# One-hots of 64 columns and a tenth run without gathers in a graph network on one core

## The chip, the cores and the metric

The kernel runs on one core of a Trainium2 chip, as one launch. The metric is the device time of that launch in microseconds (us), as the median of several runs; less is better.

## The reference

The graph has 6250 nodes with 128 features and 100000 edges, `src[e]` to `dst[e]`, sorted by `dst`. Two layers of a graph convolution come first, then a graph attention layer. Each of the two is added to its input and normalised by row.

```python
def gcn_conv(x, src, dst, ew, W, b):          # with self loops of weight 1
    deg = segment_sum(ew, dst)
    dinv = where(deg > 0, rsqrt(deg), 0)
    norm = dinv[src] * ew * dinv[dst]
    return segment_sum((x @ W)[src] * norm[:, None], dst) + b
x = layernorm(x + sigmoid(gcn_conv(relu(gcn_conv(x, .., W1, b1)), .., W2, b2)))
z, rh = x @ fc_w.T, edge_attr @ fc_r_w.T
e = leaky(z[src] @ a0 + z[dst] @ a1 + rh @ a2)
alpha = exp(e - max over dst) / sum over dst
x = layernorm(x + relu(segment_sum(alpha * (z[src] + rh), dst) + z @ loop_w))
```

## The kernel before

**Tiles, groups, banks.** Edges are cut into T = 782 tiles of 128, eight to a group (GT = 8, G = 98 groups). As `dst` is sorted, a tile's edges go to few neighbouring nodes. `base(t)` is the first of the W = 128 nodes that tile t may reach, and `rankC` holds each edge's node less that base. Sums over nodes are matmuls: the gathered rows of a tile (128 edges by 128 features) are the weights, the moving operand is a one-hot matrix S (128 edges by 128 nodes) with the edge's weight at its rank. They accumulate in a PSUM bank that holds 384 nodes and an overhang; there are NA = 17 such banks, each closed by six groups.

**Setup.** Rows of indices are turned into columns, the degrees are summed with bf16 one-hots `SH` (VectorE makes three groups of four, L1571; ScalarE the fourth, L1191 and L1195; matmuls L811), and the features are scaled by `dinv` and stored. `find_odd` (L1545 to L1562) tests whether any rank lies outside 0 to 127; if so a slow fallback runs behind everything else.

**Three passes.** Pass 0 and pass 1 are the two convolution layers, pass 2 the attention layer. GpSimd fetches the source rows, one indirect DMA for a tile (L720), into a ring of R = 18 groups (12 in pass 2). It waits for the group that it overwrites to be summed. VectorE makes S for each group (`build_S`, L1608), up to four groups ahead of TensorE; TensorE sums the eight tiles (`sum_group`, L858, in pass 2 also L860 for the edge attributes). A closed bank goes through ScalarE (`evacuate`, L1215), TensorE (`layer`, L932) and VectorE to memory; the next pass starts gathering when all banks of the one before are stored.

**Sets without gathers.** A run of 32 tiles (a set) can do without gathers, since the node rows lie in SBUF (`rows`, 49 buckets of 128 nodes). Nine sets are sorted in pass 0 by the source's bucket, four groups each, from step `MAKE[s]` on: `make_hi` (VectorE, L1627), `count_before` (TensorE, L870 to L874), `make_ranks` (VectorE, L1634 to L1650), `permute` (TensorE, L885), and at the end `unpack` (VectorE), `turn_low` (TensorE, L891), `store_low` (ScalarE). Six of them replace gathers in pass 0, all nine in pass 1, so pass 0 has 74 steps (one group each) and pass 1 has 62; three replace gathers in pass 2 in another way. A set's rows are then looked up four buckets (a chunk) at a time: SP loads the low source bits (L535), ScalarE makes a one-hot of them (`slot_onehot`, L1239 and L1241), TensorE looks up (`look_up`, L898), ScalarE copies (`copy_looked`, L1232), VectorE makes one-hots over 288 nodes (`make_slots`, L1681), TensorE sums (`sum_slots`, L910). After 13 chunks ScalarE copies the set's sum (`copy_set`, L1256) and TensorE adds it to the bank (`add_sets`, L919) in the step in which that bank closes.

The order on each engine is written out by hand, step by step; `CHUNK_AT` gives the step of each chunk, `MAKE` the first step of each set's sorting. TensorE in a step of pass 0:

```python
for m in chunks_at(0, h - 1): look_up(m)
for s_, g in made_at(h, 0): count_before(s_, g)
for s_, g in made_at(h, 3):
    if g == ST // GT - 1: turn_low(s_)
add_sets(0, h)
sum_group(0, h)
for m in chunks_at(0, h - 1): sum_slots(m)
```

VectorE in the same step: `make_hi`, `build_S`, `make_ranks`, `make_slots`, `unpack`. ScalarE: copies of the chunks of the step before, then the one-hots of this step's chunks. In pass 1 VectorE and TensorE also pick the node scores of the attention layer for each group (L1825, L944), two groups a step (`picks_at`); 72 groups are done in the pass, 26 between pass 1 and pass 2.

## Time and profile before

| | us |
|---|---|
| median of 3 runs | 2409.7 (2406.36 to 2409.96) |
| span of the profiled execution, its own time | 3348.6 |
| busy in it: TensorE, its weight loads | 2044.2, 1762.3 |
| busy: VectorE, ScalarE, GpSimd | 1834.8, 946.7, 1718.9 |
| matmuls of the groups: L858 3540, L860 1564 | 672.5, 340.3 busy |
| indirect DMAs (L720): 144 and 446 tiles in pass 0, 494 in pass 1, 686 in pass 2 | 1770 in all |

The profiled execution is one run under the profiler, and it is longer than the runs that are timed; nothing lies around its span. In the trace PE is TensorE, PEld its weight loads, DVE VectorE, ACT ScalarE, POOL GpSimd and SP the queue of loads; "L858" is a line of the kernel. A float32 matmul appears as two matmuls with two weight loads, so a group of eight tiles is x16. In brackets stands how long the engine was idle before, and what ended that.

### The profile page before, as it was taken

The page shows a single profiled execution, that of the slowest core. Times are in us where ns is not written, and L with a number is a line of the kernel's source. Part 1 is how long each engine was busy: PE and PEld are TensorE (multiplying, and loading weights), DVE is VectorE, ACT ScalarE, POOL GpSimd, SP SyncE. Part 2 cuts the span into 40 slices and gives each one's busy share as a digit, 9 for nine tenths or more (in the row PEclk, how much of TensorE's full clock was granted, in tenths as well). Part 3 has the DMA queues.
Part 4 walks back from the last instruction along what each step waited for, and adds up shares of the span by engine and source line. Part 5 has one row for each costly group of instructions (what it writes and reads, how often), then busy time and mean ns, then how long its engine had stood idle before and what let it go on. Part 6 is the DMA issues. An engine that isn't in the chain of part 4 may idle for free.

```text
span 3348.6 us, 40819 instructions
## 1 busy us (share of the span) xinstructions
PE 2044.2 (61%) x13384; PEld 1762.3 (53%) x13384; DVE 1834.8 (55%) x7005; ACT 946.7 (28%) x1754; POOL 1718.9 (51%) x1781
## 2 busy tenths in 40 slices
PE   1416444588888911177777888106677667756786
PEld 1315433566767811166666677005666666645675
DVE  3626435577779810156656687217654564546457
ACT  1316000122233300033333444101254225412541
POOL 7351666665550067466556500555766646663640
PEclk9857667798999955588988899557778778877888
DMA  4112221222221122123333332525343534443431
GB/s 118 30 42 66 69 61 47 61 61 63 60 62 32 51 76 53 41 74 86 99 103 102 93 91 80 138 62 147 97 103 97 134 93 102 108 117 79 103 97 34
DMA packets 272093, 270.54 MB, mean 81 GB/s; under 512 B 43454, under 2 KB 218709, under 8 KB 271862
## 3 DMA queue, kind: packets, MB, share of 16 engines
q1 hardware_dynamic: 201790, 143.87, 15.1%
q0 software_dynamic: 56640, 117.52, 14.8%
q10 hardware_dynamic: 13448, 6.47, 0.7%
q8 instruction: 112, 1.84, 0.2%
q14 instruction: 103, 0.84, 0.1%
HBM read 254.14 MB, written 13.97 MB: 80 GB/s over the span
## 4 chain that ended last, share of the span: by engine, by line
PE 35%; DVE 21%; another core or an unknown queue 21%; issue 15%; ACT 4%; SPq 1%; DMA 1%; POOL 1%; ACTq 0%; DVEq 0%; POOLq 0%
PE ps L858 9%; PE ps L910 8%; DVE SR L1608 5%; PE ps L860 3%; PE ps L898 3%; PE ps L1045 2%; DVE U L1709 2%; DVE SR L1681 2%; DVE SR L1571 1%; PE ps L885 1%; DVE U L1648 1%; PE ps L1029 1%; POOL ring L720 1%; PE ps L792 1%
## 5 line engine op out<-in xcount | busy, mean ns | idle before, releaser
L720 POOL DMA_INDIRECT ring<-x_d,srcC x1132 | 1109.7, 980 | 971.2 <-issue 579.0
L858 PE MATMUL ps<-SR,ring 128*128 128x128 f32 x3540 | 672.5, 320 | 205.0 <-issue 132.0
L858 PEld LDWEIGHTS ps<-SR,ring 128*128 128x128 f32 x3540 | 580.5, 231 | 238.9 <-issue 178.9
L720 POOL DMA_INDIRECT ring<-h_d,srcC x494 | 469.9, 951 | 457.1 <-DMA h_d<-Lb 170.9
L1681 DVE TENSOR_SCALAR SR<-iota_r,cols 128x288 f32<-128x288 f32 x735 | 365.0, 564 | 303.9 <-remote 226.6
L910 PE MATMUL ps<-SR 128*128 128x288 f32 x1470 | 416.6, 435 | 118.1 <-ACT SR L1232 75.3
L910 PEld LDWEIGHTS ps<-SR 128*128 128x128 f32 x1470 | 292.3, 205 | 212.7 <-ACT SR L1232 77.5
L860 PE MATMUL ps<-SR 128*128 128x128 f32 x1564 | 340.3, 312 | 40.8 <-issue 34.6
L1232 ACT COPY SR<-ps 128x512 f32<-128x512 f32 (+1 forms) x195 | 106.0, 561 | 758.4 <-remote 502.9
L860 PEld LDWEIGHTS ps<-SR 128*128 128x128 f32 x1564 | 279.6, 228 | 48.3 <-issue 48.0
L898 PE MATMUL ps<-rows,SR 128*128 128x128 f32 x1470 | 196.2, 285 | 122.5 <-ACT SR L1241 90.6
L898 PEld LDWEIGHTS ps<-rows,SR 128*128 128x128 f32 x1470 | 186.7, 200 | 134.0 <-ACT SR L1241 96.0
L1608 DVE TENSOR_SCALAR SR<-iota,rankC,ewC 128x128 f32<-128x128 f32 x940 | 253.3, 357 | 2.6 <-DVE U L1812 1.1
L1608 DVE TENSOR_SCALAR SR<-iota,rankC,cols 128x128 f32<-128x128 f32 x782 | 213.0, 355 | 14.7 <-issue 11.7
L720 POOL DMA_INDIRECT ring<-in_x_dram,srcC x144 | 137.3, 953 | 93.7 <-issue 90.5
L1571 DVE TENSOR_SCALAR SR<-iota_h,rankC 128x128 bf16<-128x128 bf16 x584 | 107.6, 260 | 125.9 <-issue 106.1
L1709 DVE SCALAR_TENSOR_TENSOR U<-SR,v2B 128x128 f32<-128x128 f32 x686 | 156.0, 286 | 34.3 <-DVE U L1709 18.1
L1239 ACT ACTIVATE SR<-SR,negp 128x512 bf16<-128x512 bf16 (+1 forms) x195 | 134.9, 692 | 112.0 <-remote 100.3
L811 PE MATMUL ps<-SR,cols 128*3 128x128 bf16 (+2 forms) x974 | 74.0, 237 | 110.7 <-issue 57.0
L1241 ACT ACTIVATE SR<-SR,negp 128x512 f32<-128x512 bf16 (+1 forms) x195 | 135.9, 697 | 6.4
L1963 DVE TENSOR_TENSOR_SCAN U<-U,ps 32x384 f32<-32x384 f32 (+2 forms) x27 | 25.4, 942 | 203.8 <-remote 115.7
L811 PEld LDWEIGHTS ps<-SR,cols 128*3 128x3 bf16 x974 | 60.0, 96 | 123.5 <-issue 65.0
(288 smaller groups left out, 2703.4 us busy)
## 6 DMA issues: line engine op xcount, KB each, us to landing
SR<-in_edge_attr_dram SPq DMA_DIRECT2D x97, 512.0 KB
SR<-low_d SPq DMA_DIRECT2D x90, 256.0 KB
U<-dlo_d SPq DMA_DIRECT2D x74, 256.0 KB
ring<-x_d,srcC POOLq DMA_INDIRECT x1132
ring<-h_d,srcC POOLq DMA_INDIRECT x494
SR<-dlo_d SPq DMA_DIRECT2D x12, 512.0 KB
ring<-in_edge_attr_dram SPq DMA_DIRECT2D x12, 512.0 KB
U<-lo_d SPq DMA_DIRECT2D x18, 256.0 KB
```

The source lines that it names most:

```text
L720: pool.indirect_dma_start(ring[:, ring_at(p, h if p < 2 else q), k, 0:width], None, (x if p == 0 and h < R0 else table)[:, :], bass.Indire ...
L811: last = nc.tensor.matmul(ps[6 + k % 2][0:3, lo:hi], ewP[:, t, :], SH[:, q % ND, j, w0:w0 + hi - lo], start=False, stop=t == LAST[k])
L858: last = nc.tensor.matmul(ps[(p * NA + k) % 2][:, at], ring[:, ring_at(p, h), j, 0:D], S[:, gg % NS, j, :], start=False, stop=stop)
L860: last = nc.tensor.matmul(ps[2 + k % 2][:, at], rh[:, q % NR, j, :], S[:, gg % NS, j, :], start=False, stop=stop)
L898: last = nc.tensor.matmul(ps[3 + m % 2][:, i * P:(i + 1) * P], ohS[:, m % 2, i * P:(i + 1) * P], rows[:, a, 0:D], start=True, stop=True)
L910: nc.tensor.matmul(ps[5][:, SLACK:SPAN], rowX[:, m % 2, i * P:(i + 1) * P], slotS[:, n % NQ, :], start=False, stop=a == NB - 1).then_inc(s ...
L1239: nc.scalar.activation(low, low, ACT.Abs, bias=negp[:, 0:1]).then_inc(s("low_apart"), 1)
L1241: return nc.scalar.activation(out, low, ACT.Relu, bias=negp[:, 1:2], scale=-1.0)
L1571: last = v.tensor_scalar(SH[:, q % ND, j, :], iota_h[:, :], rankC[:, t:t + 1], None, ALU.is_equal)
L1608: last = v.tensor_scalar(S[:, gg % NS, j, :], iota[:, :], rankC[:, t:t + 1], w[:, t:t + 1], ALU.is_equal, ALU.mult)
L1681: v.tensor_scalar(slotS[:, n % NQ, :], iota_up, slotD[:, RUNS[i], a:a + 1], slotW[:, RUNS[i], a:a + 1], ALU.is_equal, ALU.mult).then_inc(s ...
L1709: v.scalar_tensor_tensor(junk[:, n % NJ, :], attr, 1.0, v2B[:, :], ALU.mult, ALU.mult, accum_out=s2C[:, t:t + 1]).then_inc(s("rh_dotted"), 1)
```

## The change

For all but the first and the last eight tiles the one-hots are made, and the matmuls run, over the 64 columns 32 to 95 of the 128 (`view`); the test in `find_odd` uses the same bounds. Ten sets are sorted in place of nine, starting every 5 or 6 steps in place of 6, and pass 1 uses ten, which leaves it 58 steps; its chunks come at 5 steps for 12 in place of 57 for 117. Beside that: the second set buffer moves to another tile; ScalarE makes the one-hot of chunk m + 2 right after it copies chunk m; VectorE makes ranks ahead of the high parts and of S; `turn_low` moves to the end of the step before; up to four picks in a step where many are ready; the table of one bank's node scores is made after pass 1 and not in it.

```diff
+NEAR, EDGE = W // 4, GT
...
+def view(t):
+
+    return (NEAR, W - NEAR) if EDGE <= t < T - EDGE else (0, W)
...
 
     b, out = base(t), []
-    for k in range(b // BW, (b + W - 1) // BW + 1):
-        lo, hi = max(b, k * BW), min(b + W, (k + 1) * BW)
+    a, z = (b + w for w in view(t))
+    for k in range(a // BW, (z - 1) // BW + 1):
+        lo, hi = max(a, k * BW), min(z, (k + 1) * BW)
...
-SETK = (6, 8, 10, 12, 14, 15, 2, 4, 9)
-USED = ((0, 1, 2, 3, 4, 5), (6, 7, 0, 1, 8, 2, 3, 4, 5))
+SETK = (6, 8, 10, 12, 14, 15, 2, 3, 4, 11)
+USED = ((0, 1, 2, 3, 4, 5), (6, 7, 8, 0, 1, 2, 9, 3, 4, 5))
...
-NQ = 15
+NQ = 16
...
-CHUNK_AT = [[29 + m * 40 // (N0 * NC) for m in range(N0 * NC)], [1 + m * 57 // (len(USED[1]) * NC) for m in range(len(USED[1]) * NC)]]
-MAKE = [17 + 6 * i for i in range(NSET)]
+CHUNK_AT = [[29 + m * 40 // (N0 * NC) for m in range(N0 * NC)], [1 + m * 5 // 12 for m in range(len(USED[1]) * NC)]]
+MAKE = [17 + 11 * i // 2 for i in range(NSET)]
...
-        first, done = done, max(done, min(ready // 2 * 2, done + 2)) if i < HS[1] - 6 else done
+        first, done = done, max(done, min(ready // 2 * 2, done + (4 if ready - done > 12 else 2))) if i < HS[1] - 6 else done
...
-        cols = sb("cols", [P, max(2 * TC + 2, 2 * SPAN + 2 * NSET * NB)])
+        cols = sb("cols", [P, max(2 * TC + 2, SPAN + 2 * NSET * NB)])
...
-        setsum = cols[:, 0:2 * SPAN].rearrange("p (a n) -> p a n", a=2)
-        slotD, slotW = (cols[:, 2 * SPAN + k * NSET * NB:2 * SPAN + (k + 1) * NSET * NB].rearrange("p (s a) -> p s a", a=NB) for k in range(2))
+        slotD, slotW = (cols[:, SPAN + k * NSET * NB:SPAN + (k + 1) * NSET * NB].rearrange("p (s a) -> p s a", a=NB) for k in range(2))
...
+        setsum = (cols[:, 0:SPAN], Lb[:, 4, P:P + SPAN])
...
-                    at, stop = slice(column(t), column(t) + W), t + 1 in OPENS or t + 1 == T and p < 2
+                    lo, hi = view(t)
+                    at, stop = slice(column(t) + lo, column(t) + hi), t + 1 in OPENS or t + 1 == T and p < 2
                     if near:
-                        last = nc.tensor.matmul(ps[(p * NA + k) % 2][:, at], ring[:, ring_at(p, h), j, 0:D], S[:, gg % NS, j, :], start=False, stop=stop)
+                        last = nc.tensor.matmul(ps[(p * NA + k) % 2][:, at], ring[:, ring_at(p, h), j, 0:D], S[:, gg % NS, j, lo:hi], start=False, stop=stop)
                     if p == 2:
-                        last = nc.tensor.matmul(ps[2 + k % 2][:, at], rh[:, q % NR, j, :], S[:, gg % NS, j, :], start=False, stop=stop)
+                        last = nc.tensor.matmul(ps[2 + k % 2][:, at], rh[:, q % NR, j, :], S[:, gg % NS, j, lo:hi], start=False, stop=stop)
...
-                for s_, g in made_at(h, 3):
-                    if g == ST // GT - 1:
-                        turn_low(s_)
                 add_sets(0, h)
                 sum_group(0, h)
                 for m in chunks_at(0, h - 1):
                     sum_slots(m)
+                for s_, g in made_at(h, 2):
+                    if g == ST // GT - 1:
+                        turn_low(s_)
...
                 for j, t in enumerate(tiles(q)):
-                    last = nc.scalar.activation(SH[:, q % ND, j, :], iota_h[:, :], ACT.Abs, bias=rankC[:, t:t + 1], scale=-1.0)
+                    lo, hi = view(t)
+                    last = nc.scalar.activation(SH[:, q % ND, j, lo:hi], iota_h[:, lo:hi], ACT.Abs, bias=rankC[:, t:t + 1], scale=-1.0)
...
-                nc.scalar.activation(SH[:, q % ND, 0:n, :], SH[:, q % ND, 0:n, :], ACT.Relu, bias=ones[:, 0:1], scale=-1.0).then_inc(s("deg_onehot_act"), 1)
+                nc.scalar.activation(SH[:, q % ND, 0:n, lo:hi], SH[:, q % ND, 0:n, lo:hi], ACT.Relu, bias=ones[:, 0:1], scale=-1.0).then_inc(s("deg_onehot_act"), 1)
...
+                if i == 1:
+                    act.wait_ge(s("dlo_stored"), 16)
                 at = act.value_load(shift[0:1, RUNS[i]:RUNS[i] + 1], min_val=0, max_val=SLACK)
-                nc.scalar.copy(setsum[:, i % 2, :], ps[5][:, bass.ds(at, SPAN)]).then_inc(s("set_copied"), 1)
+                nc.scalar.copy(setsum[i % 2], ps[5][:, bass.ds(at, SPAN)]).then_inc(s("set_copied"), 1)
...
             def set_copies(p, h):
                 for m in chunks_at(p, h - 1):
                     copy_looked(m)
+                    if m + 2 < (len(RUNS) if p else N0) * NC:
+                        slot_onehot(m + 2)
...
             for h in range(HS[0]):
-                set_copies(0, h)
-                for m in chunks_at(0, h):
-                    slot_onehot(m)
                 for s_, g in made_at(h, 3):
                     if g == ST // GT - 1:
                         store_low(s_)
+                set_copies(0, h)
+                if h == CHUNK_AT[0][0]:
+                    slot_onehot(0)
+                    slot_onehot(1)
...
-                for m in chunks_at(1, h):
-                    slot_onehot(m)
+                if h == CHUNK_AT[1][0]:
+                    slot_onehot(N0 * NC)
+                    slot_onehot(N0 * NC + 1)
...
-                link(v.tensor_scalar(tmpC, rankC[:, :], 0.0, None, ALU.is_lt))
+                for a, z in ((0, EDGE), (EDGE, T - EDGE), (T - EDGE, TC)):
+                    last = v.tensor_scalar(tmpC[:, a:z], rankC[:, a:z], float(view(a)[0]), None, ALU.is_lt)
...
-                link(v.tensor_scalar(tmpC, rankC[:, :], float(W), None, ALU.is_ge))
+                for a, z in ((0, EDGE), (EDGE, T - EDGE), (T - EDGE, TC)):
+                    last = v.tensor_scalar(tmpC[:, a:z], rankC[:, a:z], float(view(a)[1]), None, ALU.is_ge)
...
-                    last = v.tensor_scalar(SH[:, q % ND, j, :], iota_h[:, :], rankC[:, t:t + 1], None, ALU.is_equal)
+                    lo, hi = view(t)
+                    last = v.tensor_scalar(SH[:, q % ND, j, lo:hi], iota_h[:, lo:hi], rankC[:, t:t + 1], None, ALU.is_equal)
...
-                    last = v.tensor_scalar(S[:, gg % NS, j, :], iota[:, :], rankC[:, t:t + 1], w[:, t:t + 1], ALU.is_equal, ALU.mult)
+                    lo, hi = view(t)
+                    last = v.tensor_scalar(S[:, gg % NS, j, lo:hi], iota[:, lo:hi], rankC[:, t:t + 1], w[:, t:t + 1], ALU.is_equal, ALU.mult)
...
+                for s_, g in made_at(h, 1):
+                    make_ranks(s_, g)
                 for s_, g in made_at(h, 0):
                     make_hi(s_, g)
                 build_S(0, h, wraw if h < R0 else ewC)
-                for s_, g in made_at(h, 1):
-                    make_ranks(s_, g)
...
-                        node_table(k)
+                        if k < NA - 4:
+                            node_table(k)
...
-                for k in (NA - 3, NA - 2, NA - 1):
+                for k in (NA - 4, NA - 3, NA - 2, NA - 1):
```

## Rows read from the trace of the kernel before

**Rows 1.** The chain that ended last, shares of the span by engine.
```profile
PE 35%; DVE 21%; another core or an unknown queue 21%; issue 15%; ACT 4%; SPq 1%; DMA 1%; POOL 1%; ACTq 0%; DVEq 0%; POOLq 0%
```
**Rows 2.** Timeline, early pass 1: start us, us, engine, line, operation, tiles, count, idle before.
```profile
1201.21 3.75 PE L858 MATMUL ps<-SR,ring 128*128 128x128 f32 x16 [5.12 <-DMA ring<-h_d,srcC]
...
1215.76 0.37 PE L898 MATMUL ps<-rows,SR 128*128 128x128 f32 x1 [2.43 <-issue]
...
1218.57 0.37 PE L898 MATMUL ps<-rows,SR 128*128 128x128 f32 x1 [2.43 <-issue]
```
**Rows 3.** Busy us by stretch: stretch, length, PE, PEld, DVE, ACT, POOL (counts), clock, DMA, GB/s.
```profile
25.00:296.00 271.00, 94.20 (x1091) 76.73 (x1091) 118.89 (x608) 84.90 (x213) 122.32 (x130) 0.77 0.17 44
...
1006.00:1177.00 171.00, 151.24 (x1029) 131.84 (x1027) 143.95 (x449) 58.01 (x108) 2.17 (x3) 0.97 0.14 42
...
3241.00:3349.00 108.00, 76.35 (x541) 69.80 (x541) 78.41 (x328) 20.22 (x38) 0.47 (x1) 0.86 0.17 48
```
**Rows 4.** Timeline, gathers of pass 1 (72 of them from the first to the second row).
```profile
1199.79 0.94 POOL L720 DMA_INDIRECT ring<-h_d,srcC  x1 [0.30 <-issue]
...
1289.65 0.94 POOL L720 DMA_INDIRECT ring<-h_d,srcC  x1 [0.30 <-issue]
```
**Rows 5.** Timeline, one step of pass 1 after the last gather.
```profile
1971.50 0.55 PE L944 MATMUL ps<-U 128*128 128x3 bf16 x16
...
1971.90 2.03 PE L858 MATMUL ps<-SR,ring 128*128 128x128 f32 x16
...
1972.75 3.93 DVE L1681 TENSOR_SCALAR SR<-iota_r,cols 128x288 f32<-128x288 f32 x8
...
1973.77 4.05 PE L910 MATMUL ps<-SR 128*128 128x288 f32 x16
...
1976.60 2.13 DVE L1608 TENSOR_SCALAR SR<-iota,rankC,ewC 128x128 f32<-128x128 f32 x8
...
1977.65 1.95 PE L898 MATMUL ps<-rows,SR 128*128 128x128 f32 x16
...
1979.44 0.55 PE L944 MATMUL ps<-U 128*128 128x3 bf16 x16
```
**Rows 6.** Waits of GpSimd in pass 1, 1389 to 2078: total us, times, longest.
```profile
POOL ring L720 <- PE ps L858: 115.4, 25, 29.4
```
**Rows 7.** Two widths on VectorE: one line's durations (min/median/max ns), one group of instructions.
```profile
L1617 DVE SCALAR_TENSOR_TENSOR U<-iota,rankC x9: 179/183/189, 497.7 to 1104.6; 128x32 f32<-128x32 f32 x9
...
L1709 DVE SCALAR_TENSOR_TENSOR U<-SR,v2B 128x128 f32<-128x128 f32 x686 | 156.0, 286 | 34.3 <-DVE U L1709 18.1 <-issue 6.9 <-DMA SR<-in_edge_attr_dram 5.1
```
**Rows 8.** Timeline, matmuls of 98 and of 49 moving columns.
```profile
1155.93 1.93 PE L885 MATMUL ps<-U 128*128 128x98 f32 x16
...
2415.18 1.88 PE L1029 MATMUL ps<-ring 128*128 128x49 f32 x16
```
**Rows 9.** Groups of bf16 one-hots: shapes, count, busy us, mean ns, idle before.
```profile
L1571 DVE TENSOR_SCALAR SR<-iota_h,rankC 128x128 bf16<-128x128 bf16 x584 | 107.6, 260 | 125.9 <-issue 106.1 <-remote 19.4
...
L1825 DVE TENSOR_SCALAR U<-U,pidx 128x1024 bf16<-128x1024 bf16 x74 | 33.1, 483 | 97.4 <-remote 87.2 <-PE ps L944 6.3 <-DMA U<-dlo_d 3.5
```
**Rows 10.** Timeline of sorting in pass 0, and TensorE's waits from 1006 to 1177 (last row).
```profile
1052.04 0.49 PE L870 MATMUL ps<-U,before 128*128 128x392 bf16 x1 [4.23 <-DVE U L1650]
...
1143.84 0.33 PE L870 MATMUL ps<-U,before 128*128 128x392 bf16 x1
...
1144.77 1.95 PE L858 MATMUL ps<-SR,ring 128*128 128x128 f32 x16
...
1144.97 0.57 DVE L1634 TENSOR_TENSOR U<-ps,U 128x392 f32<-128x392 f32 x1
...
1150.13 2.13 DVE L1608 TENSOR_SCALAR SR<-iota,rankC,ewC 128x128 f32<-128x128 f32 x8
...
PE ps L870 <- DVE U L1650: 10.6, 3, 4.4
```

More of the change, by code:

```diff
@@ L918, in add_sets @@
                         at = column(SAT[RUNS[i]])
-                        nc.tensor.matmul(ps[(p * NA + k) % 2][:, at:at + SPAN], ident[:, :], setsum[:, i % 2, :], start=False, stop=False
+                        nc.tensor.matmul(ps[(p * NA + k) % 2][:, at:at + SPAN], ident[:, :], setsum[i % 2], start=False, stop=False
                                          ).then_inc(s("set_added"), 1)
@@ L1548, in find_odd @@
                 link(v.tensor_reduce(odd[:, 0:1], dstF.rearrange("p b t -> p (b t)")[:, 0:T - 1], AX.X, ALU.max))
-                link(v.tensor_scalar(tmpC, rankC[:, :], 0.0, None, ALU.is_lt))
+                for a, z in ((0, EDGE), (EDGE, T - EDGE), (T - EDGE, TC)):
+                    last = v.tensor_scalar(tmpC[:, a:z], rankC[:, a:z], float(view(a)[0]), None, ALU.is_lt)
+                link(last)
                 link(v.tensor_reduce(odd[:, 1:2], tmpC[:, 0:T], AX.X, ALU.max))
-                link(v.tensor_scalar(tmpC, rankC[:, :], float(W), None, ALU.is_ge))
+                for a, z in ((0, EDGE), (EDGE, T - EDGE), (T - EDGE, TC)):
+                    last = v.tensor_scalar(tmpC[:, a:z], rankC[:, a:z], float(view(a)[1]), None, ALU.is_ge)
+                link(last)
                 link(v.scalar_tensor_tensor(tmpC, rankC[:, :], FAR / 2, tmpC, ALU.is_lt, ALU.mult))
```

## The prediction

> **What bounds the kernel now.** I read the chain of waits first. It gives TensorE 35%, VectorE 21%, an unknown queue 21% and "issue" 15% [rows 1]: no single engine, and over a third of the span in which an engine waits for nothing that can be named. The timeline shows what such time is: early in pass 1 TensorE starts one matmul in 2.8 us and waits 2.43 us before it for "issue", though sixteen take 3.75 us shortly before [rows 2]. The span is 3348.6 us and the median of the runs 2409.7 us, 938.9 us less, so most of that time must belong to the profiled execution alone. I therefore take no time from shares of the span. I take it from clean stretches, work out differences in us against the profiled execution's own rows, and carry the difference over to the median.
>
> The stretches by stage [rows 3] show where the clean ones are. From 1006 to 1177 (end of pass 0) GpSimd has finished gathering, TensorE is busy 151.2 of 171 us at clock 0.97 and VectorE 144.0: these two set the pace. The ring holds 18 groups, so a step takes about 171/18 = 9.5 us there.
>
> Then the pace of each engine in a step of pass 1. GpSimd: between the two gathers shown lie 72 intervals in 89.86 us, 1.248 us each, 0.94 busy and 0.30 idle [rows 4]. Eight are 9.98 us, 494 are 616.5 us. TensorE: a clean step [rows 5] begins with the picks at 1971.50 and the next at 1979.44, 7.94 us apart, and TensorE hardly pauses: 1.87 us for a group of eight tiles (1971.90 to 1973.77), 3.88 us for the sums of two chunks of a set (to 1977.65), 1.79 us for the look-up of the next two. So a chunk costs 2.83 us and a set of 49 buckets, 12.25 chunks' worth, 34.7 us. Pass 1 on TensorE: 62 groups x 1.87 + 9 x 34.7 + about 72 picks x 0.28 + 17 banks x 2.2 (estimate for clearing, self loops, layer) = 116 + 312 + 20 + 37 = 485 us.
>
> So if the gathers keep 1.248 us in an ordinary run, GpSimd bounds pass 1 (616 against 485). For that: all 1770 gathers x 1.248 = 2209 us, which leaves 201 us of the median for the setup that holds GpSimd up and the ends of passes. Against: in the profile GpSimd itself waits 115.4 us for TensorE in that pass, with the ring full [rows 6], and the 0.30 us gap may be the profile's. With 0.94 us alone, pass 1 would need 466 us of GpSimd, less than TensorE's 485.
>
> **The change, part by part.** *Narrow one-hots on VectorE.* Eight weighted one-hots of 128 columns take 2.13 us, eight slot rows of 288 columns 3.93 us [rows 5]: 1.41 ns a column, so 64 columns less would save 0.72 us a group. The nearest pair of narrower widths, scalar-tensor-tensor of 32 and 128 columns, 183 and 286 ns [rows 7], gives 1.07 ns and 0.55 us. The ends are 0 and 0.72; I take 0.55 as its widths enclose 64: 41 us in pass 0 (74 groups), 32 in pass 1 (58 left), 53 in pass 2 (97 narrow groups). That is busy time; what reaches the end is below.
>
> *Narrow matmuls on TensorE.* I take 0. Sixteen matmuls of 98 columns take 1.93 us and sixteen of 49 columns 1.88 [rows 8], sixteen of 128 columns 2.03 [rows 5], so the spacing doesn't follow the moving columns below 128; the 128-column weight load stays. Ends: 0 and, if the columns counted as between 128 and 288 (3.88 - 1.87 us over sixteen: 0.79 ns a column), 0.05 us for each of 3540 + 1564 matmuls. The Trainium skill, "TensorE: Matmul & The Clock Gate", section "Back-to-back issue gap", gives the spacing as growing with the moving columns, 134 cycles for 128 and about 60 for up to 64, by which the forecast would be rival C's; its section "LDWEIGHTS" ties the load to the weight's columns alone, and by that the trace agrees.
>
> *Setup.* 584 bf16 one-hots [rows 9]: 128 columns 260 ns, 1024 columns 483 ns, 0.25 ns a column, 16 ns each, 9 us in all on VectorE. ScalarE's quarter of the groups gets shorter beside it. The four more small operations of the range test cost under 1 us. Of 271 us, VectorE is busy 119 and GpSimd 122, with gathers into a ring that it can fill anyway [rows 3]; I count 7 us (0 to 15).
>
> *A tenth set sorted in pass 0.* Each of its four groups costs TensorE the counts (1143.84 to 1144.77, 0.93 us) and 16 payload matmuls (1.93): 11.4 us. VectorE pays 5.16 us a group after the counts (1144.97 to 1150.13), 21 us, against 41 saved [rows 10]. The order matters more: counting a group waits for the ranks of the group before, and TensorE sits 4.23 us there [rows 10], 10.6 us in the clean 171, which over the 53 steps of sorting (9.5 us each) is about 31 us. Ranks now come ahead of the next high parts and of the one-hots (0.6 + 2.1 us earlier), which takes 2.7 of each 4.2 us: 20 us. Queued behind the ranks is now the one-hot block, 5 us later in that step, but the group's matmuls stand behind the counts in TensorE's order anyway. The turning of a set's low half moves on TensorE from the next step's head to the end of the step of its last payload, where it waits for VectorE's unpacking, which stands behind two chunks' slot rows (3.93 us) while TensorE sums a group and two chunks (1.9 + 3.9 us): I count no wait, and 1 us for each of ten sets if VectorE is late. Queued behind it are the layer and the next step. The second set buffer's new place and the sixteenth slot row wait for nothing late. Net 11 - 20 = -9; bounds -35 (all waits gone, one-hots on the path) and +21 (nothing gained by order, low halves late). The end of GpSimd's share, 446 x 1.248 = 557 us, lies below the pass's length, so a gain here isn't cut off soon. I take -8.
>
> *Pass 1.* 32 gathers leave: 32 x 1.248 = 39.9 us off GpSimd, 462 x 1.248 = 576.6. TensorE gains 34.7 and loses 4 x 1.87: +27, to 512 us. GpSimd stays the bound, with TensorE's margin cut from 131 to 64 us. Chunks come at 2.41 a step in place of 2.05; a step with three takes 7.94 + 2.83 = 10.8 us, over GpSimd's 9.98, one with two 7.94, so the ring evens them out. Two sets now close two steps after their last chunk where three was the least, and ScalarE makes one-hots ahead of the copy that TensorE waits for there: one copy and one-hot late, some 5 us twice. In return one-hots stand ready two chunks ahead. The loads that these one-hots read keep their place on SP's queue, behind the x2 stores and pick loads of their step; a late one now holds up the set copies queued behind it on ScalarE, and then TensorE; a step has 2 us of room for that. I take -30 (bounds -42 and, with TensorE as the bound, +27).
>
> *Between the passes and pass 2.* The unfinished picks go from 26 groups to 28: two one-hot blocks, under 1 us. The one node table moved out of pass 1 lies ahead of these picks, under GpSimd's first gathers of pass 2. Pass 2 keeps 686 x 1.248 = 856 us of GpSimd; VectorE's 53 us lie beside it, except after the last gather, in the 108 us of the last stretch with its dozen groups [rows 3]: 12 x 0.55 = 7. I take -5 (0 to -20).
>
> Sum: -7 - 8 - 30 - 5 = -50 us, 2409.7 - 50 = 2360.
>
> **Rivals.** *A, the forecast:* GpSimd bounds pass 1, 2360 (own range 2325 to 2395). Chance 0.58.
>
> *B, TensorE is the bound of pass 1.* At the place where the set replaces four groups, TensorE pays 27 us more. It decides when a gather in an ordinary run takes less than 512/494 = 1.04 us: then pass 1 is TensorE's 512 after, and before it was between 485 and 512. At 0.98 us or less the price is the full 27, and with pass 0 and setup gaining little from narrower one-hots (TensorE bound there too, the sort's 11 us added, the order's 20 not needed), the total is +27 + 11 - 7 - 5 = +26: 2436; with the order's gain, 2416. For it: the 0.30 us gap and the ring-full waits [rows 4, 6]. Against: 1770 x 1.0 leaves 640 us of the median unexplained by GpSimd, while TensorE's and VectorE's clean rates don't fill it. Chance 0.15, at about 2425.
>
> *C, matmuls get cheaper with their columns.* 0.05 us x 16 x 74 = 59 us off TensorE in pass 0, of which the pass can use some 45 before GpSimd's 557 us bound it, and more margin in pass 1: 2410 - 50 - 45 = 2315. The 98- and 49-column rows speak against it. Chance 0.07.
>
> *D, the gain is eaten.* The removed gathers lie where GpSimd would wait for the ring anyway, or three-chunk steps and late set copies take the 40 us back; setup and order leave 5 to 15 us, the sort takes as much: 2405. Chance 0.20.
>
> That the change doesn't hold is excluded: outside the first and last eight tiles the reference's own destinations give ranks of 55 to 86, inside 32 to 95, so the fallback isn't entered.
>
> **How the numbers follow.** About 0.2%, 4.8 us, can be told from no change. A is faster in 0.97 of its cases, C in all, D in 0.45 (same 0.3), B in 0.05 (same 0.15): faster 0.56 + 0.07 + 0.09 + 0.01 = about 0.74, same 0.09, slower 0.17. The range runs from the middle of C to B's middle, 2315 to 2425, leaving out under 2 in 10.
>
> **What would show it.** Eight weighted one-hots near 1.58 us; sixteen 64-column matmuls still near 1.9 us; 462 gathers in pass 1 at 1.248 us; TensorE's wait for ranks down from 4.2 to about 1.5 us; the set step on TensorE unchanged. It is wrong if TensorE's granted clock in the clean stretches falls from 0.95 and more towards 0.5, where sixteen matmuls take 3.75 us [rows 2] and TensorE's share of pass 1 nearly doubles; if the gathers' interval turns out no bound; or if waits of TensorE for the set copy grow past 10 us.

## The result, and the profile after

The kernel after takes 2619.7 us (median of 6 runs, 2611.5 to 2633.8), the kernel before 2407.4 in the same session: ratio 1.088, interval 1.086 to 1.090. Forecast were 2360 us and a range of 2315 to 2425. The kernel before ran beside every group of runs below, with medians of 2406.5 to 2409.0 us; each ratio is against the one beside it, and a difference between two groups is good to some 3 us.

The span of the profile that the prediction was read from was 939 us too long, so the kernel before was profiled once more (run a1_before, 2405.6 us). First the page of the kernel after, then that of a1_before: span, busy time, TensorE's granted clock in 40 slices and the chain by engine. They answer to [rows 1].

```profile
span 2618.5 us, 41280 instructions
...
PE 2141.8 (82%) x13526; PEld 1895.1 (72%) x13526; DVE 1790.7 (68%) x7104; ACT 945.3 (36%) x1795; POOL 1722.9 (66%) x1749
...
PEclk9965668988898789988889886555786568657976
...
PE 50%; DVE 22%; POOL 12%; issue 7%; ACT 3%; DMA 3%; SPq 1%; ACTq 0%; DVEq 0%; POOLq 0%
```

```profile
span 2403.8 us, 40819 instructions
...
PE 1837.7 (76%) x13384; PEld 1625.8 (68%) x13384; DVE 1817.2 (76%) x7005; ACT 946.6 (39%) x1754; POOL 1748.7 (73%) x1781
...
PEclk9878889999999899999999995678897889779988
...
POOL 31%; DVE 24%; PE 21%; issue 15%; DMA 4%; ACT 3%; SPq 2%; ACTq 0%; POOLq 0%; DVEq 0%
```

GpSimd leads the chain before, TensorE after. TensorE is busy 304 us longer, with 1% more instructions; VectorE has lost 27 us. TensorE's mean granted clock over the span is 0.782 after and 0.878 before. The stretches of passes 0, 1 and 2, each with the pause behind it, answer to [rows 3] (length, busy time of PE, PEld, DVE, ACT and POOL, granted clock, DMA share, GB/s), the kernel after first:

```profile
147.00:902.00 755.00, 644.36 (x4007) 566.33 (x4006) 558.78 (x1792) 170.86 (x316) 483.83 (x481) 0.79 0.26 70
902.00:1621.00 719.00, 592.51 (x3728) 506.68 (x3728) 483.90 (x1605) 304.87 (x486) 445.25 (x462) 0.87 0.40 110
1621.00:2618.00 997.00, 812.61 (x4716) 746.41 (x4714) 621.52 (x2996) 387.02 (x733) 683.82 (x686) 0.68 0.47 122
```

```profile
156.00:816.00 660.00, 548.67 (x3904) 484.52 (x3903) 554.63 (x1714) 174.17 (x315) 475.58 (x474) 0.91 0.30 79
816.00:1464.00 648.00, 526.80 (x3613) 457.31 (x3614) 484.75 (x1602) 285.34 (x446) 475.99 (x494) 0.92 0.45 123
1464.00:2404.00 940.00, 668.60 (x4698) 608.40 (x4697) 641.42 (x2983) 384.24 (x733) 680.28 (x686) 0.83 0.50 129
```

Every pass is longer, at a lower clock. Pass 0 grows most (95 us); the clock falls most in pass 2, to 0.68 from 0.83, with 144 us more of TensorE for 18 instructions more.

GpSimd's timeline at the end of pass 0 (start, duration, in brackets the idle time before), first of the kernel after, then of a1_before:

```profile
775.07 0.95 POOL L727 DMA_INDIRECT ring<-x_d,srcC  x1 [0.30 <-issue]
776.32 0.95 POOL L727 DMA_INDIRECT ring<-x_d,srcC  x1 [0.30 <-issue]
902.30 0.95 POOL L727 DMA_INDIRECT ring<-h_d,srcC  x1 [125.03 <-issue]
```

```profile
773.55 0.95 POOL L720 DMA_INDIRECT ring<-x_d,srcC  x1 [0.30 <-issue]
774.81 0.95 POOL L720 DMA_INDIRECT ring<-x_d,srcC  x1 [0.30 <-issue]
816.51 0.94 POOL L720 DMA_INDIRECT ring<-h_d,srcC  x1 [40.76 <-issue]
```

The last gather of pass 0 starts at nearly the same time, 1.25 us after the one before it as in [rows 4]. The first of pass 1 comes 126.0 us later in place of 41.7: it needs the rows that pass 0 ends by storing. So GpSimd keeps its pace, and what TensorE is behind at the end of a pass becomes a pause. The starts of the gathers cut each span into six stretches, which add up to it (us):

| run | to p0's last gather | pause | pass 1's gathers | pause | pass 2's gathers | from the last on (the tail) | span |
|---|---|---|---|---|---|---|---|
| a1_before | 774.8 | 41.7 | 625.7 | 22.0 | 890.8 | 48.8 | 2403.8 |
| after | 776.3 | 126.0 | 584.9 | 134.1 | 891.9 | 105.3 | 2618.5 |
| a2_wide_all | 775.7 | 110.8 | 584.7 | 110.7 | 887.6 | 51.2 | 2520.6 |
| a3_narrow_alone | 768.3 | 55.9 | 627.7 | 23.4 | 888.8 | 103.1 | 2467.2 |
| a4_wide_matmul | 774.3 | 74.7 | 581.7 | 113.6 | 892.1 | 44.9 | 2481.3 |
| b1_order_alone | 778.0 | 56.1 | 628.0 | 24.3 | 887.1 | 48.3 | 2421.7 |
| c1_onehots_alone | 768.7 | 31.2 | 624.7 | 21.7 | 891.5 | 46.6 | 2384.4 |
| c4_matmul_32 | 765.9 | 76.1 | 623.5 | 23.5 | 908.5 | 118.8 | 2516.3 |
| d1_nine_sets | 773.8 | 37.7 | 625.5 | 21.6 | 891.6 | 47.7 | 2397.9 |
| f1_ranks_last | 768.3 | 8.4 | 625.8 | 23.1 | 890.4 | 45.2 | 2361.2 |
| g1_ten_sorted_nine_used | 769.5 | 74.9 | 623.6 | 39.1 | 895.2 | 44.9 | 2447.3 |
| h1_ten_ranks_last | 771.5 | 9.0 | 582.7 | 108.4 | 892.8 | 47.2 | 2411.6 |
| h2_after_ranks_last | 774.0 | 14.3 | 581.3 | 145.3 | 893.1 | 97.6 | 2505.6 |

Of the 214.7 us between the first two rows, the pauses take 84.3 and 112.1 and the tail 56.5; the 32 gathers left out give back 40.8.

### The profile page after: what moved, and what is told of

It is laid out like the page before. It is cut to its first block, busy times and chain, and to the rows that moved or that the text cites. A ratio compares the mean times of both kernels' runs of the same rounds, so it can differ in the third digit from the quotient of the medians.

```text
span 2618.5 us, 41280 instructions
## 1 busy us (share of the span) xinstructions
PE 2141.8 (82%) x13526; PEld 1895.1 (72%) x13526; DVE 1790.7 (68%) x7104; ACT 945.3 (36%) x1795; POOL 1722.9 (66%) x1749
## 4 chain that ended last, share of the span: by engine, by line
PE 50%; DVE 22%; POOL 12%; issue 7%; ACT 3%; DMA 3%; SPq 1%; ACTq 0%; DVEq 0%; POOLq 0%
PE ps L866 14%; PE ps L918 13%; POOL ring L727 12%; PE ps L868 5%; DVE SR L1629 4%; PE ps L906 3%; PE ps L893 3%; DVE SR L1591 3%; DVE SR L1702 3%; DVE U L1669 2%; PE ps L1053 2%; PE ps L799 1%; PE ps L1037 1%; PE ps L847 1%; DMA ring<-x_d,srcC 1%
## 5 line engine op out<-in xcount | busy, mean ns | idle before, releaser
L866 PE MATMUL ps<-SR,ring 128*128 128x64 f32 (+1 forms) x3476 | 687.2, 337 | 90.1 <-DVE SR L1629 64.8
L866 PEld LDWEIGHTS ps<-SR,ring 128*128 128x128 f32 x3476 | 618.7, 252 | 118.0 <-DVE SR L1629 70.9
L918 PE MATMUL ps<-SR 128*128 128x288 f32 x1568 | 460.7, 453 | 0.0
L918 PEld LDWEIGHTS ps<-SR 128*128 128x128 f32 x1568 | 326.6, 214 | 96.1 <-issue 4.3
L868 PE MATMUL ps<-SR 128*128 128x64 f32 (+1 forms) x1564 | 374.8, 342 | 5.7 <-DVE SR L1629 5.7
L868 PEld LDWEIGHTS ps<-SR 128*128 128x128 f32 x1564 | 316.0, 257 | 6.0 <-issue 5.8
L1629 DVE TENSOR_SCALAR SR<-iota,rankC,ewC 128x64 f32<-128x64 f32 (+1 forms) x908 | 215.1, 329 | 2.0 <-DVE U L1833 0.6
L1629 DVE TENSOR_SCALAR SR<-iota,rankC,cols 128x64 f32<-128x64 f32 (+1 forms) x782 | 185.6, 334 | 7.1 <-PE ps L868 5.7
L1248 ACT ACTIVATE SR<-SR,negp 128x512 bf16<-128x512 bf16 (+1 forms) x208 | 145.3, 698 | 11.5 <-DMA SR<-low_d 11.1
L1669 DVE TENSOR_SCALAR U<-iota,U 128x128 f32<-128x128 f32 x320 | 67.8, 297 | 107.6 <-PE ps L893 107.6
L799 PE MATMUL ps<-iota_r,zero_h 1*128 1x512 bf16 (+1 forms) x130 | 61.7, 499 | 67.5 <-DVE SR L1629 43.8
L1053 PE MATMUL ps<-ring 128*128 128x288 f32 x294 | 103.0, 505 | 0.0
```

Source lines behind the costliest of these rows:

```text
L866: last = nc.tensor.matmul(ps[(p * NA + k) % 2][:, at], ring[:, ring_at(p, h), j, 0:D], S[:, gg % NS, j, lo:hi], start=False, stop=stop)
L868: last = nc.tensor.matmul(ps[2 + k % 2][:, at], rh[:, q % NR, j, :], S[:, gg % NS, j, lo:hi], start=False, stop=stop)
L918: nc.tensor.matmul(ps[5][:, SLACK:SPAN], rowX[:, m % 2, i * P:(i + 1) * P], slotS[:, n % NQ, :], start=False, stop=a == NB - 1).then_inc(s ...
L1053: nc.tensor.matmul(ps[5][:, SLACK:SPAN], rowX2[:, m % 2, j * P:(j + 1) * P], slotX[:, n % NQ2, :], start=False, stop=a == NB - 1).then_inc ...
L1248: nc.scalar.activation(low, low, ACT.Abs, bias=negp[:, 0:1]).then_inc(s("low_apart"), 1)
L1629: last = v.tensor_scalar(S[:, gg % NS, j, lo:hi], iota[:, lo:hi], rankC[:, t:t + 1], w[:, t:t + 1], ALU.is_equal, ALU.mult)
```

## The experiments

**First split: columns, or sets and order.** The theory was that TensorE's clock falls with 64-column matmuls; the rivals, that the tenth set or the new order cost the time.

> The kernel before, once more, for a profile whose span is near its median of 2407 us (the one that the prediction was read from has 3348.6 us). All theories: span 2400 to 2460 us. If the clock theory holds, TensorE's granted clock in passes 0 to 2 is well above the 0.782 of the kernel after, 0.9 or more, and sixteen matmuls of a group mostly take near 2.0 us. If the theory of the tenth set holds (TensorE bounds pass 1 and a set costs more than four gathers), the clock is alike (0.78) and pass 1 is shorter by 30 us or more with the same pace of TensorE per instruction. If GpSimd's gathers set the pace before, their interval in this profile is near 1.25 us and TensorE's share is low.

Measured: span 2403.8 us, clock 0.878, below the 0.9 expected; the gathers of pass 1 are 1.27 us apart.

> The kernel after with one-hots and matmuls of 128 columns again (ten runs and the new order stay). Clock theory (64 streamed columns let TensorE's granted clock fall): the loss goes, 2360 to 2410 us, clock back above 0.88. Tenth-set or order theory: the loss stays, 2590 to 2650 us, clock as in the kernel after. If both parts cost, in between.

```diff
-NEAR, EDGE = W // 4, GT
+NEAR, EDGE = 0, GT
```

> The kernel before with the 64-column one-hots and matmuls alone (nine runs, old order). Clock theory: the loss is all here, 2590 to 2650 us, clock near 0.78, sixteen matmuls of a group often 3.7 us. Tenth-set or order theory: 2360 to 2400 us, since VectorE alone gets less work.

The edit: of the diff, `view`, `pieces`, the tests of `find_odd`, the slices `lo:hi` of `SH` and `S`, and those of the tile matmuls; nothing else.

> The kernel after with VectorE still writing 64 columns of a one-hot, but TensorE reading all 128 (the other 64 are cleared once, and left zero). Clock theory, if it is TensorE's own columns that count: 2340 to 2400 us, clock above 0.88. If narrower one-hots hurt in another way (VectorE running ahead, the ring emptying in bursts), or the tenth set or the order costs the time: 2590 to 2650 us as the kernel after.

```diff
-                    at, stop = slice(column(t) + lo, column(t) + hi), t + 1 in OPENS or t + 1 == T and p < 2
+                    at, stop = slice(column(t), column(t) + W), t + 1 in OPENS or t + 1 == T and p < 2
...
+            link(v.memset(S[:, :, :, :], 0.0))
```

The tile matmuls read `S[:, gg % NS, j, :]` in place of its columns `lo:hi`; a buffer that a tile of 128 columns has used is written whole once more.

Measured: a2 2526.0 us (ratio 1.050, 1.048 to 1.051), a3 2478.7 (1.030, 1.028 to 1.033), a4 2481.8 (1.030, 1.028 to 1.032). Each theory holds for a part only: sets and order cost 118 us without any narrow column, narrow columns 71 without sets and order, and giving TensorE its 128 columns back takes 138 off the whole change.

**Columns.** Does the loss lie in TensorE's columns or in VectorE's shorter work?

> The kernel before with VectorE and ScalarE writing 64 columns of a one-hot, and TensorE's tile matmuls still reading 128 (the rest cleared once). Nine sets, old order. With the matmuls narrow too this took 2479 us. Column theory (the streamed columns of the tile matmuls set TensorE's clock): 2370 to 2405 us, clock 0.87 or more. Rival (less work on VectorE lowers the clock, since TensorE then waits and works in other turns): 2450 to 2480 us, clock near 0.80.

The edit: a3 with a4's clearing of `S` and its tile matmuls over 128 columns.

> As c1_onehots_alone, but the tile matmuls read the 32 columns in which all ranks of these inputs lie (55 to 86). Column theory: the clock falls further than with 64 columns (0.795), 2500 to 2600 us. If it only matters that a matmul is below some width between 64 and 128: as with 64 columns, 2450 to 2500 us. If narrower matmuls issue faster after all: under 2400 us.

> As c1_onehots_alone, but the tile matmuls read 96 columns (16 to 111) in place of 128. By the columns streamed (128: 2388 us at clock 0.891; 64: 2479 at 0.795; 32: 2527 at 0.761) a clock near 0.84 and 2400 to 2445 us. If only columns below 65 or so lower the clock: 2385 to 2395 us.

The edits: c1 with `lo, hi = 55, 87` and `16, 112` in the tile matmuls alone.

Measured: c1 2387.8 us (0.993, 0.991 to 0.995), c2 2396.9 (0.996, 0.995 to 0.997), c4 2526.6 (1.051, 1.048 to 1.055), with a3 at 64 columns in between. c2 fell between its two expectations. The mean granted clock is 0.891 in c1 (128 columns), 0.864 in c2 (96), 0.795 in a3 (64) and 0.761 in c4 (32). Below, for c1, a3 and c4, are TensorE's groups of the tile matmuls of all passes and of the 288-column sums of slots, which no edit touches (count, busy us, mean ns, idle before).

```profile
L865 PE MATMUL ps<-SR,ring 128*128 128x128 f32 x3540 | 613.4, 305 | 107.4 <-DVE SR L1628 50.8 <-DMA ring<-h_d,srcC 23.2 <-DMA ring<-x_d,srcC 19.9
...
L917 PE MATMUL ps<-SR 128*128 128x288 f32 x1470 | 378.4, 410 | 0.0
```

```profile
L866 PE MATMUL ps<-SR,ring 128*128 128x64 f32 (+1 forms) x3540 | 667.7, 325 | 65.4 <-DVE SR L1623 30.1 <-issue 17.3 <-DMA ring<-h_d,srcC 15.6
...
L918 PE MATMUL ps<-SR 128*128 128x288 f32 x1470 | 420.4, 443 | 0.0
```

```profile
L866 PE MATMUL ps<-SR,ring 128*128 128x32 f32 (+1 forms) x3540 | 675.9, 324 | 55.6 <-issue 21.7 <-DVE SR L1629 20.6 <-DMA ring<-h_d,srcC 12.9
...
L918 PE MATMUL ps<-SR 128*128 128x288 f32 x1470 | 439.2, 457 | 0.0
```

The fewer columns the tile matmuls read, the lower the clock, and the longer the untouched matmuls too: 410, 443, 457 ns at 128, 64 and 32 columns (421 at 96). The shorter one-hots are not to blame, since c1 has them and gains. Two groups in the timeline of the kernel after, which answer to the sixteen in 2.03 us of [rows 5], show both levels, and a group of c4 the spacing of 32 columns:

```profile
311.19 3.68 PE L866 MATMUL ps<-SR,ring 128*128 128x64 f32 x16 [4.50 <-DVE SR L1629]
...
321.31 1.90 PE L866 MATMUL ps<-SR,ring 128*128 128x64 f32 x16
```

```profile
659.39 1.87 PE L866 MATMUL ps<-SR,ring 128*128 128x32 f32 x16
```

The stretches around the two of the kernel after (length, busy time of PE, PEld, DVE, ACT and POOL, then the clock) were granted 0.50 and 1.00, that is 1.2 and 2.4 GHz; ahead of the first group TensorE waited 4.50 us for one-hots.

```profile
311.00:315.00 4.00, 3.81 (x18) 3.81 (x19) 2.42 (x10) 0.09 (x1) 3.08 (x4) 0.50 0.22 56
321.00:323.30 2.30, 2.30 (x23) 2.30 (x22) 2.19 (x7) 0.00 (x0) 1.69 (x3) 1.00 0.20 50
```

Pass 2 loses most (89 us from c1 to c4). 2936 of its 4698 matmuls are tile matmuls (counts of a1_before), where in pass 0 1179 of 3904 are. Its stretches in c1 and c4:

```profile
1446.00:2384.00 938.00, 660.57 (x4699) 601.60 (x4698) 618.98 (x2983) 384.09 (x733) 682.06 (x686) 0.83 0.50 129
```

```profile
1489.00:2516.00 1027.00, 867.75 (x4690) 799.02 (x4690) 618.30 (x2983) 387.20 (x733) 680.80 (x686) 0.63 0.46 118
```

TensorE is busy 207 us longer with the same instructions, and ends 119 us after the last gather starts in place of 47.

**Order and sets.**

> The new order alone: the kernel after with 128-column one-hots and matmuls and with the nine sets, their steps and chunks of the kernel before. With the tenth set as well this took 2526 us, 118 over before, in longer pauses of GpSimd between the passes (111 and 111 us where before has 42 and 22). Tenth-set theory: the pauses go back to about 42 and 22 us, 2395 to 2420 us. Order theory (ranks first, one-hots of slots two chunks ahead, node tables later): 2460 us or more, with the first pause still near 100 us.

```diff
-SETK = (6, 8, 10, 12, 14, 15, 2, 3, 4, 11)
+SETK = (6, 8, 10, 12, 14, 15, 2, 4, 9)
-MAKE = [17 + 11 * i // 2 for i in range(NSET)]
+MAKE = [17 + 6 * i for i in range(NSET)]
```

The edit is a2 with these lines (nine sets, their old steps), and `USED` and `CHUNK_AT` of before.

> One-hots of 64 columns, tile matmuls of 128, the new order, but nine sets with the steps and chunks of before. With ten sets this took 2482 us. Tenth-set theory: 2360 to 2405 us. Order theory: 2450 us or more.

The edit: a4 with the same lines.

> As d1_nine_sets (2395 us: narrow one-hots, wide matmuls, new order, nine sets), but with VectorE's order of before in a step of pass 0: high parts, weighted one-hots, then ranks. If ranks ahead of the one-hots are what the order costs: the lag of TensorE behind the last gather of pass 0 falls from 31.5 to about 25 us and the time to 2385 to 2391 us. If another part of the order (one-hots of slots ahead of the copies, node tables, turning low halves) costs it: 2393 to 2398 us.

The edit is d1 with these lines:

```diff
-                for s_, g in made_at(h, 1):
-                    make_ranks(s_, g)
                 for s_, g in made_at(h, 0):
                     make_hi(s_, g)
                 build_S(0, h, wraw if h < R0 else ewC)
+                for s_, g in made_at(h, 1):
+                    make_ranks(s_, g)
```

Measured: b1 2427.4 us (1.009, 1.007 to 1.011), d1 2395.4 (0.995, 0.993 to 0.997), f1 2364.6 (0.983, 0.981 to 0.985). So the tenth set costs 99 us with wide one-hots (a2 less b1) and 86 with narrow ones (a4 less d1). The order as a whole costs 21 and 8. But it is two things: ranks first costs 31, and the rest gains 23 (f1 less c1), more than any theory gave it: f1 came in 20 us under its lower expectation. Waits in pass 0, between 400 and 760 us: TensorE's tile groups and counts, and VectorE's slot rows. First c1 (old order), then d1 (new order; its last row is that of the clears of banks), then f1.

```profile
L865 PE MATMUL ps<-SR,ring 128*128 128x128 f32 x512 | 67.5, 289 | 0.1
...
L877 PE MATMUL ps<-U,before 128*128 128x392 bf16 x20 | 7.2, 359 | 27.7 <-DVE U L1670 27.7
...
L1701 DVE TENSOR_SCALAR SR<-iota_r,cols 128x288 f32<-128x288 f32 x238 | 118.1, 559 | 33.5 <-PE ps L917 33.5
```

```profile
L866 PE MATMUL ps<-SR,ring 128*128 128x128 f32 x516 | 73.0, 301 | 23.9 <-DVE SR L1635 23.9
...
L878 PE MATMUL ps<-U,before 128*128 128x392 bf16 x22 | 7.2, 330 | 0.0
...
L1708 DVE TENSOR_SCALAR SR<-iota_r,cols 128x288 f32<-128x288 f32 x237 | 116.5, 558 | 0.0
...
L799 PE MATMUL ps<-iota_r,zero_h 1*128 1x512 bf16 x19 | 7.5, 394 | 11.1 <-DVE SR L1635 8.1 <-ACT cols L1267 1.5 <-ACT Lb L1267 1.4
```

```profile
L866 PE MATMUL ps<-SR,ring 128*128 128x128 f32 x550 | 74.1, 293 | 0.8 <-DVE SR L1635 0.8
...
L878 PE MATMUL ps<-U,before 128*128 128x392 bf16 x22 | 7.4, 336 | 17.0 <-DVE U L1677 16.5 <-DVE U L1654 0.5
...
L1708 DVE TENSOR_SCALAR SR<-iota_r,cols 128x288 f32<-128x288 f32 x233 | 114.5, 558 | 0.0
```

With ranks first TensorE's wait for them, that of [rows 10], goes, 27.7 to 0, and waits for the one-hots behind them take its place, 0.1 to 23.9 + 8.1. With ranks last the one-hots cost 0.8, and the ranks 17.0 in place of c1's 27.7: not gone, but less than either. VectorE's 33.5 us of waiting for sums of slots stay away in both. TensorE stands idle for 39.3, 35.0 and 22.6 of the 360 us. In f1 it ends pass 0 with the gathers: pause 8.4 us.

> As f1_ranks_last (2365 us), but ScalarE makes the one-hots of slots in their own step again, not two chunks ahead. f1 is 23 us under c1_onehots_alone, in whose pass 0 VectorE waited 33.5 us for TensorE's sums of slots between 400 and 760 us (none in f1). If the one-hots ahead bring that: 2380 to 2390 us. If the turning of the low halves in the earlier step brings it: 2362 to 2370 us.

The edit: f1 with `slot_onehot(m)` in the chunk's own step. Measured: 2370.0 us (0.984, 0.981 to 0.987). The one-hots ahead bring some 5 us, near what can be told apart. VectorE's wait for sums of slots is 0.0 in h3 too, so it isn't they that took it away. The other 18 lie with the earlier turning of the low halves and their store, or the smaller moves; these were not separated.

**Where the tenth set costs.**

> As a4_wide_matmul (2482 us: narrow one-hots, wide matmuls, ten sets), with ten sets sorted in pass 0 but the tenth not used in pass 1, whose 32 tiles are gathered again (494 gathers). If the use of the tenth set makes TensorE the bound of pass 1: TensorE's lag at the end of pass 1 falls from 91 to about 7 us, pass 1 from 673 to about 632 us, 2430 to 2445 us in all, the rest over 2395 being the sort in pass 0. If pass 1 is held up by something else of the new schedule: over 2460 us.

```diff
-USED = ((0, 1, 2, 3, 4, 5), (6, 7, 8, 0, 1, 2, 9, 3, 4, 5))
+USED = ((0, 1, 2, 3, 4, 5), (6, 7, 8, 0, 1, 2, 3, 4, 5))
```

The edit is a4 with this line.

> As a4_wide_matmul (2482 us: narrow one-hots, wide matmuls, ten sets, new order), with ranks behind the weighted one-hots as before. With nine sets that gave 2365 in place of 2395 us. If ranks first costs each pass 0 alike and the tenth set the rest: 2440 to 2455 us, pass 0's lag 30 to 45 us in place of 69, pass 1's still about 90. If the tenth set's 87 us came mostly from its sort under ranks first: under 2410 us.

> The kernel after, whole (64-column one-hots and matmuls, ten sets, new order), but with ranks behind the weighted one-hots. Ranks first then costs what it did with nine sets and wide matmuls, 30 us: 2575 to 2600 us. If TensorE at its lower clock is the bound of pass 0, so that VectorE's order no longer decides: 2610 to 2625 us.

> As h1_ten_ranks_last (2414 us: ten sets, narrow one-hots, wide matmuls, ranks last), but ranks come first in the five steps (22, 33, 44, 55, 66) in which the last group of a set and the first of the next fall together, as the sets 5 steps apart need; in h1 the high parts of the next set overwrite there what those ranks read, so five of its sets are sorted by other data. If it is the order in a step that costs, by the step: ranks first in 5 steps in place of 40 cost 5/40 of a4's 67 us over h1, 2414 to 2425 us. If h1 was fast because of its other data: 2440 to 2485 us, as a4_wide_matmul.

The edits: f1's lines in a4 (h1) and in the kernel after (h2); in h4 ranks go first in the five steps named. In h1 and h2 five of the ten sets are sorted by data that the next set has overwritten; instructions and their number stay.

Measured: g1 2453.4 us (1.020, 1.018 to 1.023), h1 2414.5 (1.004, 1.003 to 1.005), h2 2515.4 (1.046, 1.043 to 1.048), h4 2429.0 (1.009, 1.006 to 1.012). g1 was 8 us above the range that it was expected in; pass 1's denser chunks leave a pause of 39.1 without the tenth set's use. h1 and h4 show the tenth sort hidden, or nearly, with ranks last (first pause 9.0, in h4 22.4); h4 lies 4 us above the range that the order alone would give and far from a4, so it is the order, not the other data. h2 missed by 60: ranks first costs the whole change 104 us, not 30 (with the overwritten data in h2; no run did for it what h4 does for h1). Pass 0 with its pause in h1 and a4 (128 columns, ranks last and first), then in h2 (64 columns, ranks last; the kernel after, ranks first, stands among the passes above):

```profile
152.00:781.00 629.00, 536.87 (x4006) 475.22 (x4005) 557.73 (x1792) 170.68 (x316) 476.18 (x477) 0.95 0.31 82
```

```profile
152.00:849.00 697.00, 567.34 (x4007) 499.39 (x4006) 558.29 (x1792) 170.91 (x316) 478.47 (x476) 0.92 0.28 74
```

```profile
147.00:788.00 641.00, 578.06 (x4007) 515.15 (x4006) 559.54 (x1792) 170.65 (x316) 481.39 (x481) 0.87 0.31 82
```

With 128 columns ranks first make this stretch 68 us longer, and TensorE is busy for 30 of them, at a clock of 0.92 in place of 0.95. With 64 columns they make it 114 us longer, 66 of them busy, at 0.79 in place of 0.87, for the same matmuls. So more than half of what ranks first add to pass 0 of the whole change is the same matmuls running slower, and the waits and the narrow matmuls together take more off the clock than the two apart.

Pass 1 on TensorE, first f1 (777 to 1410 us), then h1 (781 to 1450): sums of slots, tile matmuls, look-ups, clears of banks.

```profile
L918 PE MATMUL ps<-SR 128*128 128x288 f32 x882 | 228.7, 412 | 0.0
...
L866 PE MATMUL ps<-SR,ring 128*128 128x128 f32 x988 | 147.3, 311 | 59.4 <-DMA ring<-h_d,srcC 44.7 <-DVE SR L1635 14.6
...
L906 PE MATMUL ps<-rows,SR 128*128 128x128 f32 x882 | 108.5, 275 | 4.1 <-ACT SR L1250 4.1
...
L799 PE MATMUL ps<-iota_r,zero_h 1*128 1x512 bf16 x26 | 10.9, 420 | 42.4 <-DMA ring<-h_d,srcC 18.9 <-DVE SR L1635 18.7 <-ACT Lb L1267 2.8
```

```profile
L918 PE MATMUL ps<-SR 128*128 128x288 f32 x980 | 256.1, 416 | 0.0
...
L866 PE MATMUL ps<-SR,ring 128*128 128x128 f32 x924 | 138.9, 314 | 22.3 <-DVE SR L1635 13.2 <-DMA ring<-h_d,srcC 8.9
...
L906 PE MATMUL ps<-rows,SR 128*128 128x128 f32 x980 | 128.2, 283 | 36.4 <-ACT SR L1250 36.4
...
L799 PE MATMUL ps<-iota_r,zero_h 1*128 1x512 bf16 x27 | 11.2, 415 | 40.8 <-DVE SR L1635 27.0 <-ACT cols L1267 6.2 <-ACT Lb L1267 6.0
```

In f1 TensorE waits 44.7 + 18.9 = 63.6 us for gathers: that is all its slack. The tenth set adds 27.4 us of sums and 19.7 of look-ups, and takes off 8.4 of tile matmuls; look-ups wait 32.3 us more for ScalarE's one-hots (28.9 stand in g1's trace too, with nine sets in the denser chunks), and clears 17.3 us more for VectorE and ScalarE (40.8 against 42.4 less 18.9). TensorE then ends 87 us after the last gather starts (in f1 7), where 43 us of gathers were saved.

**A version that beats both.** f1_ranks_last, 42 us under before. Whether its clearing of the buffers costs anything was tried on c1: in c5 the first use of each buffer writes all 128 columns instead.

> As c1_onehots_alone (2388 us, 0.993 of before), but instead of clearing the one-hot buffers once, the first use of each writes all 128 columns. The first tile matmul of c1 came at 151.5 us of its span, that of the kernel with narrow matmuls, which clears nothing, at 146.9. If the clearing delays pass 0 and GpSimd's gathers with it: 2381 to 2386 us. If the start of pass 0 is covered by the ring and only its end counts: 2386 to 2391 us.

c5 took 2391.3 us (0.993, 0.992 to 0.995), as c1: pass 0's first tile matmul starts 4.5 us earlier (147.0 in place of 151.5), but its last gather does not (772.9, in c1 768.7).

## Why the prediction was wrong

Along one path of medians the loss, some 213 us, reads: narrow one-hots on VectorE -19 (before to c1), the order without ranks first -23 (to f1), the tenth set +50 (to h1), narrow tile matmuls +101 (to h2), ranks first +104 (to the kernel after). On other paths the parts weigh differently (narrow matmuls 91 in a3 less c1, ranks first 31 in d1 less f1), because TensorE's slack can be spent once, and because columns and waits lower the clock together.

- *What bounds the kernel.* Right for the kernel before: GpSimd's gathers at 625.7 us over 493 intervals, 1.27 us each, against 1.248 forecast from the inflated profile.
- *Narrow matmuls on TensorE, "I take 0".* The step that failed first. The spacing did stay, as the rows said: 1.90 us for sixteen at the high level. By that the trace agrees with the Trainium skill, "TensorE: Matmul & The Clock Gate", section "LDWEIGHTS (loading the stationary operand)", by which the load goes by the weight's columns. The figure of some 60 cycles for up to 64 columns is that of an isolated matmul: the Trainium skill, same page, section "Back-to-back issue gap", says itself that such figures are too low for a stream of weight loads and matmuls at few columns, which the prediction left out. The loss came by the clock, 0.795 in place of 0.891 from c1 to a3: 91 us alone, 101 on the path above. I bounded the cost at 0 and a gain, never a loss, though the text ends by naming a fall of the clock as what would make it wrong. It should have been a rival with a price: [rows 2] had the 3.75 us.
- *VectorE.* Weighted one-hots fell from 363 to 328 ns (below, a1_before and the kernel after), 0.28 us a group, not 0.55. The pair of scalar-tensor-tensor rows was the wrong neighbour. Setup gained 8.7 us (first tile matmul at 155.6, then 146.9) where I said 7, but no run shows that it reaches the end; in c5 a start 4.5 us earlier than c1's did not.

```profile
L1608 DVE TENSOR_SCALAR SR<-iota,rankC,ewC 128x128 f32<-128x128 f32 x940 | 256.4, 363 | 2.2 <-DVE U L1812 0.5
```

```profile
L1629 DVE TENSOR_SCALAR SR<-iota,rankC,ewC 128x64 f32<-128x64 f32 x884 | 208.7, 328 | 2.0 <-DVE U L1833 0.6
```

- *Order, -20.* Wrong in sign for ranks first. The wait it removes was larger than read (62.9 us over pass 0 of a1_before, from 156 to 816 us, not 31) and did go; I dismissed what is queued behind ("the group's matmuls stand behind the counts in TensorE's order anyway"), and that became the new wait: ranks first cost 31 us with nine sets and 104 in the whole change, where the clock fell with it. The turning of the low halves, counted at 0 to +1 us a set, belongs to what gained 23.
- *The tenth set.* Its sort alone costs next to nothing with ranks last (I said +11): from f1 to h1 pass 0 with its pause ends 3.9 us later. In pass 1 the -30, with GpSimd as the bound and 64 us of margin left to TensorE, failed: TensorE's 485 us came from one clean step with two chunks, extended over the pass. From pass 1's first gather to its last tile matmul f1 takes 632.7 us, less 63.6 of waiting for gathers 569, and h1 669.3 less 8.9, 660; so the set costs 91 with its waits, not 27. TensorE's margin was 64 us in f1, and in the kernel before 44 (19.6 + 24.6 below, a1_before from 816 to 1449 us), not 131. This is rival B's mechanism, but B was tied to gathers under 1.04 us; it decided at 1.27. Rival C is refuted by c4, D by its size, as the pauses alone grew by 196 us.

```profile
L858 PE MATMUL ps<-SR,ring 128*128 128x128 f32 x988 | 145.1, 308 | 52.0 <-DVE SR L1608 32.2 <-DMA ring<-h_d,srcC 19.6
...
L792 PE MATMUL ps<-iota_r,zero_h 1*128 1x512 bf16 x26 | 10.7, 413 | 44.2 <-DMA ring<-h_d,srcC 24.6 <-DVE SR L1608 15.1 <-ACT cols L1256 3.8
```

- *Pass 2, -5.* Without narrow matmuls near that (tail 46.6 in c1, 48.8 before); with them the tail took 56 us more.

## What to carry to other kernels

Where one engine runs ahead through a deep ring, a slower second engine need not hold it up inside a pass (in the kernel after GpSimd waited 1.8 us in all for sums of TensorE); the lag comes out as a pause at the end, so take the second engine's slack from what it waits for the leader over a whole pass, not from one clean step. Narrow what VectorE writes and leave the matmul its zero columns, where the spacing hardly shrinks with them (here 1.90 against 1.95 us for sixteen). Before a block is moved ahead of another, ask who waits for the block that is now behind.

## What was unexpected of the hardware

Matmuls with nearly the same spacing at the high level (sixteen in 1.87 us at 32 columns, 1.90 at 64, 1.95 at 128) ran at clocks of 0.891, 0.864, 0.795 and 0.761 on the whole with 128, 96, 64 and 32 columns read, although TensorE's busy share did not fall (70% of pass 2 in c1, 84% in c4, where the slower clock itself makes it busier), and matmuls beside them slowed with them. That the columns lower it is shown by c1, c2 and c4, which differ in nothing else, and a3, which lacks only the clearing of `S` and the writes that go with it. They are not all of it: with the columns unchanged, ranks first and its waits took pass 0 from 0.87 to 0.79 (h2 to the kernel after). How the chip decides was not tried.
